# Linear-attention layer: key features begin after two blocks are projected, the other projections move between them through one spare PSUM bank

## The reference

```python
qkv = layernorm(x) @ W_qkv.T              # q, k, v: 16 heads of 8
q_p = elu(einsum(q, proj)) + 1            # 128 features for each head
k_p = elu(einsum(k, proj)) + 1
kv = einsum('bhnf,bhnd->bhfd', k_p, v)    # sum over all 2048 tokens
attn = einsum('bhnf,bhfd->bhnd', q_p, kv) / (q_p . sum_n k_p)
x = x + attn @ W_out.T + b_out
```

## Time and profile before

| | |
|---|---|
| median of 3 runs | 593.04 us (592.62 to 594.12) |
| the profiled execution | 591.61 us, its span 589.7 us |
| busy share of PE / DVE / ACT / POOL | 67% / 51% / 41% / 38% |
| first experts' rows landed | 306.7 us |
| first key features on PE | 331.95 us |
| key loop on PE (32 steps) | 336.5 to 376.1 us |
| query features and router | 376 to 474 us |

### The profile page before, as it was taken

The page is one execution under the profiler, slowest core; times in us unless marked ns, Lnnn a source line. Parts: engine busy times, 40 slices in busy tenths (PEclk is TensorE's granted clock), DMA queues, the critical chain, the costliest instruction groups (busy, mean ns, idle before and its releaser), DMA issues.

```text
span 589.7 us, 6529 instructions
## 1 busy us (share of the span) xinstructions
PE 393.6 (67%) x2200; PEld 261.9 (44%) x2200; DVE 298.4 (51%) x693; ACT 239.3 (41%) x340; POOL 224.6 (38%) x246
## 2 busy tenths in 40 slices
PE   2827686767540019999907899977777406999960
PEld 1435444325330017888804533333334304888840
DVE  5486999919462001231128699876685511121213
ACT  2836334343430013332314799868567402233210
POOL 4001888810055686455433100000415360545450
PEclk9959888786655559999966999987877556999985
DMA  7970000000361121212042444440001011221108
GB/s 192 350 222 2 0 1 0 0 0 2 102 215 41 45 87 38 72 53 73 28 135 60 105 97 102 95 143 2 25 12 37 23 45 51 71 65 60 50 34 217
DMA packets 40562, 43.49 MB, mean 74 GB/s; under 512 B 5840, under 2 KB 27984, under 8 KB 40528
## 3 DMA queue, kind: packets, MB, share of 16 engines
q1 hardware_dynamic: 31696, 32.50, 19.4%
q0 software_dynamic: 4608, 8.47, 4.2%
q10 hardware_dynamic: 4224, 2.10, 1.4%
HBM read 17.72 MB, written 20.07 MB: 64 GB/s over the span
## 4 chain that ended last, share of the span: by engine, by line
PE 41%; DVE 13%; issue 11%; ACT 6%; DMA 5%; POOL 4%; POOLq 0%; SPq 0%; DVEq 0%; ACTq 0%
PE ps L1064 38%; DVE feat L989 3%; POOL slots_x L448 3%; DMA got<-chosen_y 2%; PE ps L1211 2%; ACT expo L664 1%; DMA slots_x<-rows_x,put_at 1%; ACT L664 1%; ACT rows_x L593 1%; POOL chosen_y L480 1%; DMA chosen_y<-ye,y_to 1%; DVE stats L816 1%; DVE otok L728 1%; DVE stats L720 1%; DVE chosen L838 0%
## 5 line engine op out<-in xcount | busy, mean ns | idle before, releaser
L448 POOL DMA_INDIRECT slots_x<-rows_x,put_at x64 | 62.8, 981 | 165.2 <-DVE put_at L866 118.9
L480 POOL DMA_INDIRECT chosen_y<-ye,y_to x80 | 78.3, 979 | 84.8 <-DVE ye L930 62.7
L623 ACT ACTIVATE hT<-ps 128x640 f32<-128x640 f32 x64 | 45.1, 704 | 98.7 <-issue 63.2
L989 DVE SCALAR_TENSOR_TENSOR feat<-expo,ps 128x1024 f32<-128x1024 f32 x64 | 76.8, 1216 | 12.2 <-ACT expo L664 11.5
L1064 PE MATMUL ps<-xeT,cfc_sb 128*128 128x320 f32 x256 | 75.7, 451 | 2.0 <-DVE xeT L908 2.0
L664 ACT ACTIVATE expo<-ps,minus_one 128x1024 f32<-128x1024 f32 x64 | 70.3, 1114 | 13.3 <-PE ps L1064 9.5
L1064 PE MATMUL ps<-cproj_sb,hT 128*128 128x128 f32 x640 | 74.6, 275 | 0.3
L908 DVE COPY xeT<-ps 128x640 f32<-128x640 f32 x16 | 13.2, 824 | 121.3 <-PE ps L1211 64.6
L1064 PEld LDWEIGHTS ps<-cproj_sb,hT 128*128 128x128 f32 x640 | 73.0, 192 | 0.9 <-ACT hT L623 0.6
L1064 PEld LDWEIGHTS ps<-xeT,cfc_sb 128*128 128x128 f32 x256 | 47.7, 199 | 24.1 <-ACT hT L623 6.3
L1211 PE MATMUL ps<-ident,xe 128*128 128x128 f32 x80 | 12.5, 292 | 55.6 <-DMA xe<-slots_x 55.6
(11 more groups left out here) (192 smaller groups left out, 638.2 us busy)
## 6 DMA issues: line engine op xcount, KB each, us to landing
stk<-part SPq DMA_DIRECT2D x96, 64.0 KB, 2.0
slots_x<-empty_rows SPq DMA_DIRECT2D x16, 325.0 KB, 7.4
xe<-slots_x SPq DMA_DIRECT2D x16, 325.0 KB
chosen_y<-empty_rows SPq DMA_DIRECT2D x16, 256.0 KB
cfc_sb<-in_L_ffn_c_fc SPq DMA_DIRECT2D x2, 2048.0 KB, 8.9
got<-chosen_y ACTq DMA_DIRECT2D x8, 256.0 KB, 5.8
got<-chosen_y SPq DMA_DIRECT2D x8, 256.0 KB, 5.9
chosen_y<-ye,y_to POOLq DMA_INDIRECT x80
```

The lines of the kernel that those rows point to most:

```text
L448: pool.indirect_dma_start(out=slots_x[k], out_offset=bass.IndirectOffsetOnAxis(ap=put_at[:, c, kk, t:t + 1], axis=0), in_=rows_x[:, kk * N ...
L480: pool.indirect_dma_start(out=chosen_y[k], out_offset=bass.IndirectOffsetOnAxis(ap=y_to[:, b, i:i + 1], axis=0), in_=ye[:, b, i * D:(i + 1 ...
L623: act.activation(hT[:, b, f, :].rearrange("p (a n) -> p a n", a=2), ps[:, 2 + 2 * (f % 2):4 + 2 * (f % 2), 0:HALF], ACT.Gelu).then_inc(h_r ...
L989: dve.scalar_tensor_tensor(out=feat[:, g % 4, :], in0=expo[:, g % 3, :], scalar=1.0, in1=flat(ps[:, pair, :]), op0=ALU.min, op1=ALU.max).t ...
```

## The change

Only the projections of blocks 0 and 1 stand before the features, and of those only keys and values. The rest moves into the key loop: after `key_values(s)` PE turns, or projects, one block through bank 7 (`SIDE`) if a table has a row for `s`. That bank is free because the sums of even and odd steps now share bank 6, 256 columns each. ACT and DVE get their copies and remainders at fixed steps of their own loops. The rows of `xn` are now written by ACT (`norm_rows`), from a `shift` that DVE computes; the four roots stand ahead of the features, and an exponential of one column (`spare`) makes ACT load the table of the exponential before the first features are there. Keys come ahead of values in the first two blocks.

```diff
+EARLY = 2
+TURN_IN = {1: 2, 8: 3}
+KEY_IN = {3: 2, 10: 3}
+VALUE_IN = {6: 2, 13: 3}
+QUERY_IN = {15: 0, 18: 1, 21: 2, 24: 3}
+SIDE = 7
...
             for g in range(NK + 2):
                 feature_exp(g, pair_of(g - NK))
+                if g - 1 in TURN_IN:
+                    norm_rows(TURN_IN[g - 1])
+                if g - 3 in TURN_IN:
+                    copy_turned(TURN_IN[g - 3], SIDE)
+                if g - 3 in KEY_IN:
+                    copy_keys(KEY_IN[g - 3], SIDE)
+                if g - 3 in VALUE_IN:
+                    copy_values(VALUE_IN[g - 3], SIDE)
+                if g - 3 in QUERY_IN:
+                    copy_queries(QUERY_IN[g - 3], SIDE)
             act.wait_ge(kv_mm, NK)
-            copy(kv_sb[:], ps[:, 6:8, 0:2 * F]).then_inc(kv_copied, 1)
+            copy(kv_sb[:].rearrange("p a f -> p (a f)"), ps[:, 6, :]).then_inc(kv_copied, 1)
...
             for g in range(NK + 2):
                 feature(g, pair_of(g - NK))
+                if g - 3 in KEY_IN:
+                    low_part(KEY_IN[g - 3], 0, SIDE, khi2_ready, klo2_ready)
+                if g - 3 in QUERY_IN:
+                    low_part(QUERY_IN[g - 3], 1, SIDE, qhi2_ready, qlo2_ready)
...
+            turn_chunk(0, 0)
+            project_keys(0, 4)
+            project_values(0, 2)
+            turn_chunk(1, 1)
+            project_keys(1, 5)
+            project_values(1, 3)
...
             def key_values(s):
                 t, gp = divmod(s, 2)
+                pe.wait_ge(v2_ready, t // TB + 1)
                 pe.wait_ge(f_ready, s + 1)
                 for cg in range(4):
-                    ins = mm(ps[32 * cg:32 * cg + 32, 6 + gp, 0:2 * F], vaug[:, t, 4 * gp + cg, :],
-                             feat[:, s % 4, cg * 2 * F:(cg + 1) * 2 * F], start=t == 0, stop=t == NT - 1,
+                    ins = mm(ps[32 * cg:32 * cg + 32, 6, 2 * gp * F:2 * (gp + 1) * F], vaug[:, t, 4 * gp + cg, :],
+                             feat[:, s % 4, cg * 2 * F:(cg + 1) * 2 * F], start=s == 0, stop=s == NK - 1,
                              tile_position=(0, 32 * cg))
...
-            pe.wait_ge(v2_ready, NB)
-            pe.wait_ge(klo2_ready, NB)
-            for s in range(3):
-                key_features(s)
-            pe.wait_ge(qlo2_ready, NB)
+            pe.wait_ge(xnT_ready, 2 * NB + EARLY)
+            key_features(0)
+            pe.wait_ge(v2_ready, EARLY)
+            key_features(1)
+            pe.wait_ge(klo2_ready, EARLY)
+            key_features(2)
             for _ in range(24):
                 pe.transpose(ps[:, 7, 0:P], xn[:, 0, :], ident[:])
             for s in range(NK):
...
                 key_values(s)
-
+                if s in TURN_IN:
+                    turn_chunk(TURN_IN[s], SIDE)
+                if s in KEY_IN:
+                    project_keys(KEY_IN[s], SIDE)
+                if s in VALUE_IN:
+                    project_values(VALUE_IN[s], SIDE)
+                if s in QUERY_IN:
+                    project_queries(QUERY_IN[s], SIDE)
```

More of the change, by code:

```diff
@@ L643, in _, with norm_rows, copy_turned, copy_values @@
             experts(0)
-            ln_root(3, 0)
-            for c in range(NB):
-                cc = slice(c * BK, (c + 1) * BK)
+            def norm_rows(c):
+                act.wait_ge(ln_shift, NB + c + 1)
+                for t in range(TB * c, TB * c + TB):
+                    act.activation(xn[:, t, :], xres[:, t, :], ACT.Identity, scale=rstd[:, t:t + 1],
+                                   bias=shift[:, t:t + 1]).then_inc(ln_out, 1)
+            def copy_turned(c, bank):
                 act.wait_ge(xn_turned, 3 * NB + c + 1)
-                copy(xnT[:, cc], ps[:, c % 2, :]).then_inc(xnT_ready, 1)
-                if c + 1 < NB:
-                    ln_root(3, c + 1)
+                copy(xnT[:, c * BK:(c + 1) * BK], ps[:, bank, :]).then_inc(xnT_ready, 1)
+            def copy_values(c, bank):
                 act.wait_ge(v2_mm, c + 1)
                 copy(vaug[:, TB * c:TB * c + TB, :, 0:PAIR].rearrange("p t r (a e) -> p (t r) a e", a=2)[:, :, :, 0:HD],
-                     ps[:, 2 + c % 2, :].rearrange("p (r a d) -> p r a d", a=2, d=HD)).then_inc(v2_ready, 1)
+                     ps[:, bank, :].rearrange("p (r a d) -> p r a d", a=2, d=HD)).then_inc(v2_ready, 1)
+            def copy_keys(c, bank):
                 act.wait_ge(k2_mm, c + 1)
-                copy(part[:, 0, 0, cc], ps[:, 4 + c % 2, :]).then_inc(khi2_ready, 1)
+                copy(part[:, 0, 0, c * BK:(c + 1) * BK], ps[:, bank, :]).then_inc(khi2_ready, 1)
+            def copy_queries(c, bank):
                 act.wait_ge(q2_mm, c + 1)
-                copy(part[:, 1, 0, cc], ps[:, 6 + c % 2, :]).then_inc(qhi2_ready, 1)
+                copy(part[:, 1, 0, c * BK:(c + 1) * BK], ps[:, bank, :]).then_inc(qhi2_ready, 1)
+            ln_root(3, 0)
+            norm_rows(0)
+            ln_root(3, 1)
+            copy_turned(0, 0)
+            norm_rows(1)
+            copy_keys(0, 4)
+            copy_turned(1, 1)
+            ln_root(3, 2)
+            copy_values(0, 2)
+            copy_keys(1, 5)
+            ln_root(3, 3)
+            copy_values(1, 3)
+            act.activation(spare[:], minus_one[:], ACT.Exp)
             def feature_exp(g, pair):
@@ L939, in mix, with mix_rows @@
                                   ALU.add).then_inc(mix_first, 1)
+            def mix_rows(k, c):
                 dve.wait_ge(mix_first, k * NB + c + 1)
                 rows = flat(xres[:, TB * c:TB * c + TB, :])
-                dve.tensor_tensor(rows, rows, first, ALU.add).then_inc(mixed, 1)
+                dve.tensor_tensor(rows, rows, flat(got[:, TB * c:TB * c + TB, :]), ALU.add).then_inc(mixed, 1)
             experts(0)
@@ L958, in norm_chunk, with low_part @@
                 dve.wait_ge(ln_rstd, rooted(3, c))
[L959 to L963, removed]
+                dve.scalar_tensor_tensor(out=shift[:, tt], in0=mv[:, tt, 0], scalar=-1.0, in1=rstd[:, tt],
+                                         op0=ALU.mult, op1=ALU.mult).then_inc(ln_shift, 1)
+            def low_part(c, n, bank, hi_ready, lo_ready):
                 cc = slice(c * BK, (c + 1) * BK)
                 dve.wait_ge(hi_ready, c + 1)
-                dve.tensor_tensor(part[:, n, 1, cc], ps[:, 4 + 2 * n + c % 2, :], part[:, n, 0, cc].bitcast(F32),
+                dve.tensor_tensor(part[:, n, 1, cc], ps[:, bank, :], part[:, n, 0, cc].bitcast(F32),
                                   ALU.subtract).then_inc(lo_ready, 1)
-            mix(0, 0)
+            mix_pair(0, 0)
+            mix_rows(0, 0)
             stats_chunk(0)
[L971 to L981, removed]
+            norm_chunk(0)
+            mix_pair(0, 1)
+            mix_rows(0, 1)
+            stats_chunk(1)
+            norm_chunk(1)
+            mix_pair(0, 2)
+            mix_rows(0, 2)
+            stats_chunk(2)
+            low_part(0, 0, 4, khi2_ready, klo2_ready)
+            norm_chunk(2)
+            mix_pair(0, 3)
+            mix_rows(0, 3)
+            stats_chunk(3)
+            low_part(1, 0, 5, khi2_ready, klo2_ready)
+            norm_chunk(3)
             def feature(g, pair):
@@ L1247, in _, with turn_chunk @@
             experts(0)
-            def turn_chunk(c):
-                if c >= 2:
-                    pe.wait_ge(xnT_ready, 2 * NB + c - 1)
+            def turn_chunk(c, bank):
+                if c == EARLY:
+                    pe.wait_ge(v2_ready, EARLY)
+                if c > EARLY:
+                    pe.wait_ge(v2_ready, c)
                 for t in range(TB * c, TB * c + TB):
                     pe.wait_ge(ln_out, 3 * NT + t + 1)
-                    ins = pe.transpose(ps[:, c % 2, (t % TB) * P:(t % TB + 1) * P], xn[:, t, :], ident[:])
+                    ins = pe.transpose(ps[:, bank, (t % TB) * P:(t % TB + 1) * P], xn[:, t, :], ident[:])
@@ L1255, in turn_chunk, with project_keys, project_values @@
                 ins.then_inc(xn_turned, 1)
-            def project(c):
-                cc = slice(c * BK, (c + 1) * BK)
+            def project_keys(c, bank):
                 pe.wait_ge(xnT_ready, 2 * NB + c + 1)
-                if c >= 2:
-                    pe.wait_ge(v2_ready, c - 1)
+                mm(ps[:, bank, :], wkT[:], xnT[:, c * BK:(c + 1) * BK]).then_inc(k2_mm, 1)
+            def project_values(c, bank):
+                if c >= EARLY:
+                    pe.wait_ge(klo2_ready, c + 1)
@@ L1262, in project @@
                 for t in range(TB * c, TB * c + TB):
-                    ins = mm(ps[:, 2 + c % 2, (t % TB) * P:(t % TB + 1) * P], xnT[:, t * P:(t + 1) * P], wvT[:])
+                    ins = mm(ps[:, bank, (t % TB) * P:(t % TB + 1) * P], xnT[:, t * P:(t + 1) * P], wvT[:])
                 ins.then_inc(v2_mm, 1)
[L1265 to L1276, removed]
+            def project_queries(c, bank):
+                if c:
+                    pe.wait_ge(qlo2_ready, c)
+                else:
+                    pe.wait_ge(v2_ready, NB)
```

(1 more changed line is left out.)

10 lines of the change are left out of this document (7 added, 3 removed).

## The result

| | before | changed |
|---|---|---|
| median of 12 runs | 592.95 us (591.62 to 597.15) | 596.0 us (594.1 to 599.8) |
| ratio, with its 95% interval | | 1.0042 (1.0023 to 1.0062) |
| profiled execution, its span | 591.61, 589.7 us | 596.34, 594.4 us |

The change makes the kernel slower by 3.05 us in the medians. The forecast was slower by 3.85, to 596.9.

The account below looks back on a forecast made before the run. PE was taken to bound the key loop: a loop start 4.05 us earlier against 7.9 us of side jobs makes +3.85 us, median 596.9 us. The 8-in-10 range was 592.6 to 600.0 us.

Parts of the forecast that it names:

- The bound of the loop: Key loop: PE sets the pace at 1.233 us a step; DVE alone needs 1.13, ACT 1.00.
- The rival that DVE is the bound: Key loop: PE's jobs hide, only DVE's 4.1 us add; 593.1 us, no change; chance 0.08.
- Earlier keys: Before the loop: first transfer at 317.0, first feature product near 326.0, 5.95 us earlier than 331.95.
- Side jobs: Key loop: turns and value, key and query projections on PE add in full, 7.9 us.
- ACT, DVE, transfers, one bank, costed at nothing: Key loop: added ACT and DVE work hides, transfers land in time, the shared bank for sums costs nothing.
- Table load: Before the loop: moving the 1.28 us load into the transfer wait gains nothing, since the 24 transposes take longer.
- The clock: Before the loop: PE's clock falls while it waits, slowing the burst; loop begins at 332.5, gain 4.05 us.
- With 4.8: Before the loop: the clock returns 4.8 us into the burst, which takes 6.5 us.
- both bounds: Start of the key loop: between 332.0 and 333.0, around the estimate of 332.5.
- The query part, which I take as unchanged: Behind the key loop: everything just moves by +3.85 us, with no change in its own length.
- a sign that it was wrong: Query part: clock changes elsewhere and a move of more than a microsecond would show the forecast wrong.
- the forecast's own range: Kernel time if the main forecast holds (chance 0.66): 595.3 to 599.4 us.

Follow-up runs that it names:

- e2: Changed kernel with each of its four query projections issued twice on PE; ratio 1.0098, loop 50.71 us.
- e1: Kernel before with the changed one's extra key-loop work on DVE and ACT, none on PE; ratio 1.0046, loop 43.25 us.
- e3: Changed kernel without the one-column exponential ahead of the features; loop began at +26.50 and took 47.28 us, no kernel time given.
- e8: Changed kernel with half the first block's `stk` transfers issued by ACT and 12 instead of 24 unread transposes; 593.07 us, 0.9993 of before.
- e9: Changed kernel with the first block's `stk` transfers issued by SP, ACT and GpSimd, and 8 instead of 24 unread transposes; 1.0012 of before.
- e4: Changed kernel with 20 more unread transposes on PE in its wait for the `stk` transfers; 1.0028 of before.
- e6: Changed kernel with query projections of blocks 0 and 1 moved from the loop into PE's wait for transfers; 1.0008 of before.
- e10: Three-queue transfer kernel with block 0's query projection replacing the unread transposes, other side jobs one or two steps later; 593.04 us, 0.9995 of before.
- e7: Changed kernel with half the first block's twelve `stk` transfers issued by ACT instead of SP; 590.99 us in a single run.

## Why the prediction was right

**The bound of the loop.** Right: e2 adds what its matmuls take, e1 shows DVE's own pace of 1.13 us under the load. The rival that DVE is the bound, and with it the rule of the Trainium skill (page "Perfetto Trace Analysis", section "Identifying the Most-Contended Engine") to judge PE by its MFU (the share of peak arithmetic) and its weight loads, would have led to a forecast of no change. The MFU isn't worked out here; weight loads fill 19.4 of the loop's 47.4 us, DVE 40.6, and PE's list sets the time all the same.

**Earlier keys.** Right: the first transfer at +10.23 (forecast 317.0 - 306.7 = +10.3), the first product at +19.36 (+19.3).

**Side jobs.** Right: 47.29 - 39.50 = 7.8 us against 7.9.

**ACT, DVE, transfers, one bank, costed at nothing.** Right: PE has no wait in the loop, and one step is 0.08 us longer than its jobs. e1 shows that this held only because PE got slower.

**Table load.** Right (e3): without the early load the first feature came 1.27 us later, and the loop began where it did. The Trainium skill (page "ScalarE: Activation LUTs", section "What ACT_TABLE_LOAD costs") gives about 1.28 us for the load and 1.38 for a drain, 2.66 in all. The load agrees with the row; of the drain e3 shows nothing. With quicker transfers (e8, e9) the load is on the path again, as the timeline of e8 shows.

**The clock.** The fall was right, and e4 shows it by taking it away: 3.2 us. Its size is the term that I missized. "With 4.8" us to come back it would have been a start at 332.5, +25.8; it took 6.7 (327.79 to 334.5), beyond both bounds, and the loop began at +26.58. So the stage grew by 4.5 instead of 3.85 us. Both bounds had been counted from PE's first projections or products. PE had come back earlier each time, with transposes, in the trace of before:

```profile
311.13 1.57 PE L1254 MATMUL ps<-ident,xn 128*128 128x128 f32 x4 [14.94 <-DVE xn L960]
...
490.63 1.30 PE L1211 MATMUL ps<-ident,xe 128*128 128x128 f32 x5 [18.12 <-DMA xe<-slots_x]
```

From these the clock took 8.1 us (to 319.2) and 6.1 us (to 496.7), and 6.7 lies between. Even so the rows of one trace don't bound it: in the changed kernel's own first block it took 12.0 us from PE's first transposes (+3.92) to the rise (+15.9).

**What follows.** "The query part, which I take as unchanged" was the assumption that failed, on the side of a faster kernel: it gave back 1.5 us, with other clock changes. The prediction had named a move of more than a microsecond there as a sign that it was wrong, and that sign came. 4.5 - 1.5 = 3.0 us is what the medians show. The two errors, 0.7 and 1.5, partly cancel. That the forecast 596.9 lies within 0.9 us of the measured 596.0 is in part luck.

**The range.** By its own terms (0.5 + 0.5 + 0.3 us below 596.9) the forecast's own range starts at 595.6, not at 595.3.

## What to carry to other kernels

Where three engines look full in a loop, compare distances, not busy shares: the pace each keeps when it works off a stock, and which one starts late after its input is ready. Work moved under that one's loop isn't hidden but only moved; and a start made earlier is worth less if it opens a wait of PE in which its clock falls. Work put into that wait counted twice here: it left the loop and kept the clock.

## What I had not expected

The clock changes of the query part are repeated by a kernel (18.2 us after the copy of the sums in both profiles of before, 27.3 in both of the changed kernel), and shift a part that wasn't touched by 1.5 us. It doesn't explain why the stage shortened by 0.4 to 1.0 us (e6, e8, e10) didn't show in the time: in the profiles of e8 and e10 the part from the copy on took 209.2 and 209.9 us, as before. The intervals of the times, 1.2 to 1.6 us to either side, are too wide for such a gain. Also, the clock came back 6.7 us after PE resumed, within 0.1 us of the same place in both profiles of the changed kernel (+26.1 and +26.2 from DVE's first add), though that add itself moved by 1.9 us. It isn't always so repeatable: e7 and e8 run the same list up to the first product, and their clock came back at +19.3 and +11.9.
